# An attention and expert kernel on one core: the first normalised rows are stored, loaded back in quarters and turned in VectorE's blocks, the gate moves one place later, and reciprocals are taken for two heads at a time

## What is computed

```python
q, k, v = layernorm(x) @ wq.T + bq, ctx @ wk.T + bk, ctx @ wv.T + bv   # 32 batches, 256 rows, 512 features, 16 heads of 32
scores = where(mask, q @ k.T / sqrt(32), -1e9)
x = x + (softmax(scores) @ v) @ wo.T + bo
xf = layernorm(x)                                                        # 8192 rows
gate = softmax(xf @ w_gate); weights, idx = top_k(gate, 2)               # 8 experts, capacity 2048
h = xf[rows of the expert] @ c_fc; h = silu(h[:, :768]) * h[:, 768:]
x = x + sum over the two experts of weight * (h @ c_proj)
```

## Time and profile before

| | |
|---|---|
| profiled execution | 2922.17 us, span 2920.3 us |
| median of 3 runs | 2912.38 us |
| attention and routing | first 1300 us or so of the span |
| experts | from there on, bound by PE without gaps |
| steady step of the attention | some 39 us |
| PE clock granted | 1.00 of full speed in nearly every stretch of the attention |

### The profile page before, as it was taken

One profiled execution on the slowest core, in us unless ns is written; L12 is line 12 of the kernel. 1 busy time (PEld: TensorE's weight loads), 2 busy tenths in 40 slices (PEclk: granted clock), 3 DMA queues, 4 the chain that ended last, 5 costly groups with the idle time before them and its releaser, 6 DMA issues.

```text
span 2920.3 us, 53159 instructions
## 1 busy us (share of the span) xinstructions
PE 2791.5 (96%) x17472; PEld 2273.4 (78%) x17472; DVE 1592.8 (55%) x5156; ACT 1374.0 (47%) x3628; POOL 1278.3 (44%) x1920
## 2 busy tenths in 40 slices
PE   6999999999999999967999999999999999999998
PEld 5777777777777777746888888888888888888886
DVE  6888888888888888863333232242332332423331
ACT  5767777667777776743232232232322322323321
POOL 5677777777777776652212121222121212121201
PEclk9999999999999999978999999999999999999999
DMA  4344444444444443425444343434343434343412
GB/s 147 106 119 123 131 124 127 120 109 122 122 129 129 125 124 107 113 81 160 94 87 94 80 102 77 104 76 97 83 91 83 94 85 88 90 89 91 73 32 29
DMA packets 247367, 296.30 MB, mean 101 GB/s; under 512 B 40384, under 2 KB 159168, under 8 KB 245568
## 3 DMA queue, kind: packets, MB, share of 16 engines
q1 hardware_dynamic: 184032, 159.58, 21.1%
q0 software_dynamic: 32768, 67.26, 13.3%
q10 hardware_dynamic: 30304, 66.07, 6.8%
HBM read 125.26 MB, written 67.90 MB: 66 GB/s over the span
## 4 chain that ended last, share of the span: by engine, by line
PE 53%; DMA 1%; issue 0%; ACT 0%; POOL 0%; DVE 0%; SPq 0%; POOLq 0%
PE a_ps L1659 18%; PE g_ps L1659 18%; PE y_ps L1674 18%; DMA fc_raw<-in_c_fc 1%; DMA out<-y,recs 0%; DMA xg<-xn_rows,lists 0%; POOL xg L1452 0%; DMA lists<-table 0%; ACT fc_hi L1515 0%; POOL out L1500 0%; ACT L1555 0%; DVE hidden L1622 0%; ACT y L1571 0%; ACT act_part L1555 0%; SPq L1394 0%
## 5 line engine op out<-in xcount | busy, mean ns | idle before, releaser
L1500 POOL DMA_INDIRECT out<-y,recs x128 | 205.2, 1603 | 1184.3 <-ACT y L1571 863.4
L427 POOL TENSOR_SCALAR probs<-probs,row_inv 128x256 f32<-128x256 f32 x1024 | 506.1, 509 | 298.7 <-DVE row_inv L775 285.0
L1622 DVE TENSOR_TENSOR hidden<-act_part,g_ps 128x512 f32<-128x512 f32 x192 | 132.1, 688 | 893.6 <-ACT act_part L1555 893.6
L570 ACT ACTIVATE probs<-probs,low 128x256 f32<-128x256 f32 x1024 | 511.6, 503 | 193.4 <-DVE low L766 124.8
L766 DVE CUSTOM_DVE_ANT_0 probs<-scores_ps,mask_add,row_any 128x256 f32<-128x256 f32 x1024 | 429.6, 477 | 17.5 <-remote 14.8
L1659 PE MATMUL a_ps<-xe_hi,fc_hi 128*128 128x512 f32 x768 | 300.2, 391 | 4.6 <-DVE xe_lo L1578 2.6
L1674 PE MATMUL y_ps<-pj_hi,ht_hi 128*128 128x512 f32 x768 | 299.5, 390 | 0.7
L1659 PE MATMUL a_ps<-xe_lo,fc_hi 128*128 128x512 f32 x768 | 299.7, 390 | 0.0
L1659 PE MATMUL a_ps<-xe_hi,fc_lo 128*128 128x512 f32 x768 | 299.7, 390 | 0.0
L1674 PE MATMUL y_ps<-pj_hi,ht_lo 128*128 128x512 f32 x768 | 298.9, 389 | 0.0
L1674 PE MATMUL y_ps<-pj_lo,ht_hi 128*128 128x512 f32 x768 | 298.8, 389 | 0.0
(11 more groups left out here) (204 smaller groups left out, 6472.7 us busy)
## 6 DMA issues: line engine op xcount, KB each, us to landing
probs_m<-blocks SPq DMA_DIRECT2D x1024, 64.0 KB
x_quarters<-xg SPq DMA_DIRECT2D x496, 64.0 KB
fc_raw<-in_c_fc SPq DMA_DIRECT2D x24, 1024.0 KB, 5.7
out<-x_xn ACTq DMA_DIRECT2D x32, 512.0 KB, 2.8
xn_rows<-x_xn ACTq DMA_DIRECT2D x32, 512.0 KB
cin<-in_ctx_t ACTq DMA_DIRECT2D x31, 512.0 KB, 6.2
xin<-in_x ACTq DMA_DIRECT2D x31, 512.0 KB, 4.4
quarters<-xn_rows SPq DMA_DIRECT2D x120, 128.0 KB
```

The lines of the kernel that those rows point to most:

```text
L427: last = nc.gpsimd.tensor_scalar(probs[:, r, t, :], probs[:, r, t, :], row_inv[:, r, t:t + 1], 1.0, ALU.mult, ALU.mult)
L570: last = nc.scalar.activation(probs[:, r, t, :], probs[:, r, t, :], ACT.Exp, scale=-1.0, bias=low[:, r, t:t + 1], accum_out=row_sum[:, r, ...
L1500: nc.gpsimd.indirect_dma_start(out=out[:, :], out_offset=bass.IndirectOffsetOnAxis(ap=recs[:, i * CT + t, 0:1].bitcast(U32), axis=0), in_= ...
L1622: nc.vector.tensor_tensor(hidden[:, m % 2, :], act_part[:, m % 2, :], g_ps[m % 2][:, :], ALU.mult).then_inc(gated, 1)
```

## The change

`xn` is no longer turned by PE. SP stores it to a new array in HBM (`store_xn`), loads it back in quarters into the buffer `quarters` that the second layernorm uses too (`quarters_x`), and DVE turns it in four transposes back into `xn`, now called `x_turned` (`turn_x`). The features come out in another order, so the rows of the query weights are laid out in that order on the host. Since `quarters` has two users, `quarters_x` waits for `turn_x2` of the same step and stands between the halves of the first `move`; `quarters_x2` waits for `turn_x` of the step before. `normalise_x` moves to the head of DVE's step, and the moments and the root of the first layernorm are taken one step earlier (`xin` has three buffers instead of two). `gate` and `gate_sum` of PE move behind the first half of `outputs` and its `probs_turn`, and `gate_out` of ACT behind the second head's exponents. `invert` takes two heads in one reciprocal, behind the four `mask_scores` for the first pair, and waits for the second head's exponents.

```diff
+                def store_xn(b):
+                    sp.wait_ge(xn_ready, b + 1)
+                    sp.dma_start(xn_out[b], xn[:, :, :]).then_inc(xn_stored, 16)
+                def quarters_x(b):
+                    sp.wait_ge(xn_stored, 16 * (b + 1))
+                    need(sp, x2t_ready, (b - 2) * TILES)
+                    for a in range(GROUPS):
+                        sp.dma_start(quarters[a * DK:(a + 1) * DK, :, :], xn_quarters[b, a]).then_inc(x_quartered, 16)
...
-                        if c == 0 and has(n + 1) and n >= 0:
-                            root(0, n + 1, ln1_var, ln1_chain, ln1_rstd, xn_ready)
+                        if c == 0 and has(n + 2) and n >= -1:
+                            root(0, n + 2, ln1_var, ln1_chain, ln1_rstd, xn_ready)
...
+                        if r == 1 and late:
+                            gate_out(n - 2)
+                        if r >= 2 and proj and n >= 0:
+                            x_hi(n + 1, r - 2)
                         if heads:
                             turned_out(g + 1, r)
...
                 def invert(g):
-                    dve.wait_ge(exped, g + 1)
-                    nc.vector.reciprocal(row_inv[:, r, :], row_sum[:, r, :]).then_inc(inverted, 1)
+                    dve.wait_ge(exped, g + 2)
+                    nc.vector.reciprocal(row_inv[:, r:r + 2, :], row_sum[:, r:r + 2, :]).then_inc(inverted, 2)
...
-                            if r >= 2:
-                                invert(g * HPC + r - 2)
+                        invert(g * HPC)
...
                     if heads:
                         scores(g + 2)
                     if proj and n >= 0:
-                        x_lo(n + 1, 1)
+                        turn_x(n + 1)
...
-                        if n >= 0:
-                            x_turn(n + 1, 0)
...
-                    if late:
-                        gate(n - 2)
-                    if proj and n >= 0:
-                        x_turn(n + 1, 1)
                     for t in range(TILES):
                         for half in range(HALVES):
+                            if late and t == 0 and half == 1:
+                                gate(n - 2)
                             if tail:
                                 outputs(n - 1, t, half)
-                            if late and t == 0 and half == 0:
+                            if late and t == 0 and half == 1:
                                 gate_sum(n - 2)
                             if heads:
                                 probs_turn(g + 1, t * HALVES + half)
```

More of the change, by code:

```diff
@@ L69, in settle, with attention_block @@
     eng.nop(nofuse=True)
[L72 removed]
+def attention_block(nc, x, ctx_t, mask, w_attn, b_qk, b_v, b_o, w_gate, out, xn_rows, xn2_rows, table):
     from contextlib import ExitStack
@@ L186, in attention_block @@
         defaults_stored = sem("defaults_stored")
-        x_loaded = [sem(f"x_loaded{i}") for i in range(2)]
+        x_loaded = [sem(f"x_loaded{i}") for i in range(3)]
         c_loaded = sem("c_loaded")
@@ L300, in quarters_x2, with move @@
                         sp.dma_start(quarters[a * DK:(a + 1) * DK, :, :], xn2_quarters[b, a]).then_inc(x2_quartered, 16)
-                def move(g):
+                def move(g, parts):
                     need(sp, attended, g - 1)
-                    for a in range(GROUPS):
+                    for a in parts:
                         settle(sp)
@@ L334, in _ @@
                 for n in range(BATCH):
+                    if has(n + 1):
+                        store_xn(n + 1)
                     if has(n - 2):
                         quarters_x2(n - 2)
-                    move(n * DC)
-                    move(n * DC + 2)
+                    move(n * DC, (0, 1))
+                    if has(n + 1):
+                        quarters_x(n + 1)
+                    move(n * DC, (2, 3))
+                    move(n * DC + 2, range(GROUPS))
                 sp.wait_ge(defaults_stored, 16 * (EXPERTS + 2))
@@ L577, in step @@
                     if n == -2:
-                        for t in range(TILES):
-                            x_hi(0, t)
                         weights_hi(0)
                         weights_hi(1)
+                        for i in range(2):
+                            x_hi(0, i)
                     g, h = n * DC, n * HEADS
@@ L648, in step @@
                         qk_out(0, n + 1, 1, bank_c)
-                    if has(n + 2) and n >= -1:
-                        load_x(act, n + 2)
+                    if has(n + 3):
+                        load_x(act, n + 3)
                     if has(n + 3):
@@ L716, in normalise_ordered, with turn_blocks, turn_x @@
                         rstd[:, 1, t:t + 1], ALU.subtract, ALU.mult).then_inc(ordered_ready, 1)
+                def turn_blocks(dst, done):
+                    for c in range(DC):
+                        last = nc.vector.transpose(dst[:, c, :].rearrange("p (g l) -> p g l", l=DK),
+                                                   quarters[:, :, c * DK:(c + 1) * DK])
+                        if c % 2:
+                            last.then_inc(done, 1)
+                def turn_x(b):
+                    dve.wait_ge(x_quartered, 16 * GROUPS * (b + 1))
+                    turn_blocks(x_turned, xt_full)
                 def turn_x2(b):
@@ L894, in step @@
                         normalise_x(0)
-                        for t in range(TILES):
-                            x_lo(0, t)
                         split_w(0)
@@ L910, in step @@
                         dve.wait_ge(pool_const, 11)
+                        turn_x(0)
+                        for i in range(2):
+                            x_lo(0, i)
                         split_w(1)
@@ L929, in step @@
                     if heads:
-                        invert(g * HPC + 3)
-                    if proj and n >= 0:
-                        normalise_x(n + 1)
+                        invert(g * HPC + 2)
                     if heads:
@@ L942, in step @@
                         invert(g * HPC + HPC + 2)
-                    if proj and n >= 0:
-                        x_lo(n + 1, 0)
-                    if heads:
-                        invert(g * HPC + HPC + 3)
                     if late:
@@ L952, in step @@
                     if proj and n >= 0:
-                        x_lo(n + 1, 1)
+                        turn_x(n + 1)
+                    if tail:
+                        x2_out(n - 1, 0)
                     if late:
                         logits_out(n - 2)
-                    if tail:
-                        x2_out(n - 1, 0)
+                        route(n - 2)
                     if heads:
                         invert(g * HPC + 2 * HPC + 2)
-                    if late:
-                        route(n - 2)
-                    if heads:
-                        invert(g * HPC + 2 * HPC + 3)
+                    if proj and n >= 0:
+                        for i in range(2):
+                            x_lo(n + 1, i)
                     if tail:
@@ L1204, in places @@
                     pe.wait_ge(member_ready, b + 1)
-                    if has(b + 3):
-                        pe.wait_ge(xt_split, (b + 4) * TILES)
+                    need(pe, place_used, b)
                     need(pe, route_step, b * 16)
```

93 lines of the change are left out of this document (40 added, 53 removed).

## The result

| | before | after |
|---|---|---|
| median of 4 runs | 2912.14 us (2908.65 to 2918.61) | 3039.05 us (3036.02 to 3047.54) |
| ratio | | 1.0429 (95% interval 1.0410 to 1.0448) |
| profiled execution, span | 2922.17 us, 2920.3 us | 3039.18 us, 3037.4 us |

The change costs 127 us by the medians; the forecast was 68. The experts take as long as before: the last second normalisation stands at 1301.04 us in the trace before and at 1416.18 after, 115.1 of the 117.1 by which the span grew. So all but 2 us of it is lost in the attention.

A forecast was written before the change was run, and what follows sets the result against it. The prediction took a slackless ring through DVE, ACT and POOL as the bound: 1.02 + 1.4 - 0.94 + 0.5 + 0.2 = +2.2 us a step, times 30 is 66, plus 2 for start-up, giving 2980 us; range 2915 to 3050.

The forecast's parts named there:

- The ring: Relay of DVE's masks, ACT's exponents and POOL's scalings, claimed without slack and as long as the step; +2.2 us a step.
- link 1: On DVE, second normalisation to masks of g: `normalise_x` now stands between, +1.02 us, bounds 1.0 and 1.1.
- link 2: Masks of g to turn of g: third head, root and fourth head follow the reciprocal, +1.4 us, bounds +0.9 and +1.9.
- link 3: Masks of g+1 to those of g+2: `x_lo` and its wait for `x_hi` go, -0.94 us, bounds -0.94 and -0.4.
- link 4: Masks of g+2 to turn of g+2: exponents sooner, two heads scaled instead of one, +0.5 us, bounds -0.5 and +1.2.
- 5 and turns: Turn of g+2 and masks of g+3 to the second normalisation: no change or up to +0.5 us, +0.2 taken.
- the cover in link 4: ACT's 5 us from last mask to last exponents hide `turn_x`, `x_lo`, outputs and routing; uncovered, `turn_x` would cost 1.4.
- rule on breaking up instructions: Splitting helps where VectorE is unsaturated but causes bubbles; by it the pairs cost time, 0.3 us a step without them, not 2.2.
- SP's queue: Slower rival: moves on SP's queue land twice as late, 4.8 us after issue; 66 us more, 3046 us; chance 0.12.
- one sign that the prediction named for it: `attend(g)` on PE waiting for `probs_m` in most steps; the prediction would then be wrong.
- PE is the bound: Faster rival: PE's list sets the step, which falls by 2.28 us to 2844 us total; decides under 38; chance 0.14.
- What would show it: Expected signs: step near 41.3 us, turn of g some 10.5 behind first mask, PE at most 90%, gaps at most some 1.5.

The follow-up runs named there:

- e2: Changed kernel with the first layernorm's root on POOL moved behind the fourth head's scaling of chunk g: 3012.80 us.
- e9: Changed kernel without `x_lo` from batch 1 on, so the queries use the low parts of batch 0: 3007.25 us.
- e11: Kernel before with both the two-head reciprocals and the later place of `gate`, `gate_sum` and `gate_out`: 2978.82 us, ratio 1.0243.
- e7: Changed kernel with single reciprocals, root behind the fourth head's scaling, `normalise_x` a step earlier, and `turn_x`, `x_hi`, `x_lo`, store and loads moved: 2902.32 us, ratio 0.9949.
- e1: Changed kernel with one reciprocal for each head again, in the order of the kernel before: 2983.18 us, ratio 1.0252.
- e8: Changed kernel with `turn_x` behind the routing and both `x_hi` behind the fourth head's exponents: 3030.90 us.
- e3_gate: Changed kernel with `gate`, `gate_sum` and `gate_out` back at their places in the kernel before: 3066.16 us.
- e5_pairs: Kernel before with the reciprocals of two heads alone, at the places of the changed kernel: 3076.58 us, ratio 1.0550.
- e10_records: Changed kernel with single reciprocals, POOL's four records in the bias addition's place and that addition behind the second layernorm's root: 3052.13 us.

## Why the prediction was right, and where its size was off

**Right in kind.** The ring through DVE, ACT and POOL set the step, and the change lengthened it. No busy time explains the loss, while edits that touch a single piece of the ring move the step by about that piece: the root off it takes 1.0 off the step (e2), `x_lo` 0.8 (e9), and the pairs put onto the kernel before add 2.7 (e11). With the pieces off the ring the turned path is no slower than before (e7). Single reciprocals (e1) took 3.1 off two links, but only 1.7 off the step.

**Link by link**, forecast and measured difference to before:

| link | forecast | measured | |
|---|---|---|---|
| 1 | +1.02 | +1.24 | `normalise_x` takes 1.31, not 1.09: it starts while a scaling runs on POOL |
| 2 | +1.4 | +1.44 | third head, root, fourth head in a row |
| 3 | -0.94 | -0.90 | |
| 4 | +0.5 | +1.63 | see below |
| 5 and turns | +0.2 | +0.25 | |

They add up to +2.2 and +3.66. Over the 29 steps from the second normalisation at 105.08 to that at 1243.20 before, and from 113.99 to 1357.95 after, the mean step is 39.25 and 42.90, so 106 us; another 8.9 are lost ahead of them, where I had put 2 for the start-up. Which part of the start-up costs this, no experiment separates. That 3039 still lies inside the range is in part luck: links 1 and 4 came out above their own bounds (1.1 and 1.2), and only because links 2, 3 and 5 kept clear of theirs does the sum stay under the 4.3 of all bounds together.

**The step that failed is the cover in link 4**: "`turn_x` ..., `x_lo`, the outputs and the routing run while ACT works through link 4, whose 5 us from the last mask to the last exponents cover them". The exponents end where I had them (8.4 behind the first mask forecast; 922.79 - 914.42 = 8.4 in the step shown). But `turn_x` waits for its quarters, the routing behind it ends late, and the reciprocal comes 8.97 behind the first mask, 0.5 late. And `x_lo` is not under the exponents: it needs the high parts that ACT makes between and behind them, and stands behind the reciprocal, so it lies beside the pair's scaling, and two heads take 2.64 instead of 1.88. 0.5 + 0.76 is the miss: link 4 is 926.40 - 914.42 = 11.98 in this step, 1.28 over the 10.7 forecast. e9 shows the second part as a cause: without `x_lo` link 4 is 0.88 shorter, and the turn comes 2.2 behind the reciprocal (medians 10.97 and 8.75), as forecast with 2.24; e8 shows that the first alone gives nothing, as long as `x_lo` then lies beside the scaling for all its length.

The row that could have told it was there: in the earlier trace rows a scaling beside `normalise_x` takes 1.37, others 0.94. I used it for a bound of link 2 and not for `x_lo`, which until then read one of its two inputs from PSUM (`bank_a`) and now reads both from SBUF (`xn` and `xt_hi`, 923.48 above). In the step of the kernel before:

```profile
633.83 0.69 DVE L750 TENSOR_TENSOR xt_lo<-bank_a,xt_hi 128x512 fp32r<-128x512 f32 x1 [0.69 <-ACT xt_hi L499]
```

The Trainium skill has a rule for such a pair ("SBUF — State Buffer", SBUF: two separate sides): VectorE and GpSimd share a pair of ports, an instruction of VectorE with two inputs from SBUF takes it whole against one of GpSimd that reads SBUF, and the other engine waits. The trace agrees: 2.64 beside `x_lo`, 1.85 without it.

**The pairs.** The forecast "with single reciprocals links 2 and 4 would be 0.94 shorter each" came out as 1.89 and 1.22, but 1.54 was lost again ahead of the masks of g+1, and 52 us came back where 1.88 x 30 = 56 were worked out: a sum that is nearly right from parts that are not. The Trainium skill's rule on breaking up instructions, cited in the prediction, held: pairs cost 85 us in e11_pairs_gate.

**The gate.** Its move was the one part that pays: 14 us by itself, 33 in the changed kernel, where it keeps PE's clock up (e3_gate). I had counted the waits that it moves and not the clock, which falls in every step when the pairs come without it (e5_pairs).

**The rivals.** *SP's queue* did not take the place, although one sign that the prediction named for it came: `attend(g)` waited for `probs_m` in most steps, 22 of them, 18.3 us in total. It started 8.8 behind the first mask of g+2 in the step above (923.21), where 9.9 was forecast (whose terms add up to 9.7), and waited 0.24 there for the last move to land. The sign was the wrong one, since such a wait costs only what reaches DVE: its masks waited 2.7 us for scores in the whole run, and in steps 5 to 29 those of g+3 started at least 2.1 behind the end of their own scores, where a mask that does wait starts 0.9 behind it (e7_step_later). Wait list, one step, page row:

```profile
PE attn_ps L1125 <- DMA probs_m<-blocks: 18.3, 22, 2.6
```

```profile
923.21 1.07 PE L1125 MATMUL attn_ps<-probs_m,v 128*32 128x256 f32 x16 [0.24 <-DMA probs_m<-blocks]
```

```profile
L798 DVE CUSTOM_DVE_ANT_0 probs<-scores_ps,mask_add,row_any 128x256 f32<-128x256 f32 x1024 | 420.5, 474 | 2.7 <-PE scores_ps L1142 2.7
```

*PE is the bound* did not hold in the changed kernel, at 87%; in e7_step_later, at 98% of a step of 37.6, it is close to it, near the 38 from which I had it decide. The 0.92 read for the first `x_turn` holds an idle time of 0.41, and PE is busy 1.01 less in e7's step than in the earlier trace rows, not 1.33 less:

```profile
632.54 0.38 PE L1030 MATMUL bank_a<-ident,xn 128*128 128x128 f32 x2 [0.41 <-issue]
```

**What would show it.** The order of instructions, `gate_sum` behind `gate_out`, PE under 90% and the turn 10.5 behind the first mask (905.51 - 895.04 = 10.47) came as said; the step of 41.3 and gaps of 1.5 at most did not (42.57, and 1.90 ahead of the next scores), and only the first of the three gaps above 1 us stands ahead of a `probs_turn`; the other two wait for ACT.

## What to carry to other kernels

Where four engines hand work round in a ring, price an edit by what it adds between one hand-over and the next, and ask of each instruction that is said to be covered when its own input is there: `x_lo` cost no time of the ring on VectorE and 0.9 us of it on GpSimd. The price of one edit can hang on another, since a wait on TensorE may also cost its clock: the pairs cost 85 us with the later gate and 160 without it. And a saving on the busiest engine (the transposes taken off TensorE) gains nothing while the ring is longer than that engine's list.

## What was not expected of the hardware

- Scores that end beside GpSimd's indirect DMAs can reach VectorE late: 2.4 us from the end of the matmul to the start of the mask in e1_single (827.76 to 830.18), 49.7 us over that run. In most steps the wait ends with the third record, and the waits went along when the records were moved (e10_records), which speaks for the records as a cause. It is not shown that they are the only one, nor by which path: in the kernel before, two masks of g+2 waited 1.1 and 1.6 us in the same way with no record near.
- A scaling on GpSimd (1.85 us for two heads) takes 2.64 to 2.86 beside a subtraction on VectorE with both inputs in SBUF. VectorE's normalisation takes 1.31 where it starts while a scaling runs (893.80), and 1.09 where it starts just ahead of one (892.79, the scaling from 892.85 on); no run has it alone.
- A wait of 2.67 us on TensorE in each step (e5_pairs) went with a granted clock of 0.50 in each step; a wait of 2.0 us in each step (e3_gate) did so in 20 of 26 only.
